# Cross-attention scores from two float32r parts in the 64-row halves of TensorE, in place of three bfloat16 parts in 99 rows

## The chip, the cores and the metric

One core of a Trainium2 chip runs the whole program. The metric is the time of one execution in device microseconds. Three runs of the kernel before gave 1007.08, 1010.96 and 1012.14 us; the median, 1010.96 us, is what the change is measured against.

## What is computed

Two decoder layers on x [2, 512, 256] with a context [2, 1024, 256]. The change touches the two cross-attentions. Cut to them:

```python
# layer 0: keys and values from all 1024 rows of the context, 16 heads of 16
q = split_heads(x_norm @ wq.T + bq); k = split_heads(ctx @ wk.T + bk); v = split_heads(ctx @ wv.T + bv)
p = softmax(where(mask, q @ k.T / 4, -inf)); out = (p @ v) @ wo.T + bo
# layer 1: one key and one value head of 16 for each batch, shared by the 16 query heads,
# from 512 rows of the context, chosen by an exact argmax
p = softmax(q @ k.T / 4); out = (p @ v) @ Wc.T
```

All inputs are float32, and the scores are wanted at nearly float32 accuracy.

## The kernel before

The stages run one after another: Mamba, first cross-attention (`cross_stage`, L1380), experts, shared-key attention, second cross-attention (`hard_cross_stage`, L2112), experts. Both cross-attentions use the class `Attention` (L919).

**Units.** The work is cut into eight units: a batch and a group of four heads (GH = 4). For each unit a query buffer Qs holds 99 partitions x 4 heads x 512 queries in bfloat16, and a key buffer Ks 99 partitions x 4 heads x 1024 keys (in the second attention one head, 512 keys). A float32 number is written as three bfloat16 parts p0 + p1 + p2. The 99 rows are six blocks of 16 (the head's dimensions), which pair the parts so that one matmul sums the six products that matter, and three tail rows, which carry the mask and, in the second pass, minus the row maximum. SyncE fills the blocks by DMA from the part tiles KP and QP (`key_part` L1472, `query_part` L1478) and the tail rows from DRAM or from `ktail` (`tails`, L1465); each DMA counts on the semaphore `loaded`.

**Two passes for each unit.** TensorE makes the scores twice. `scores` (L969, matmul L980) gives 128 queries x 512 keys; VectorE takes the row maxima of each bank (`maxima`, L1075, tensor_reduce L1080). When a unit's maxima are there, `negated` (L1083) writes minus the maximum as two bfloat16 values into MT, TensorE transposes MT (`maxima_transposes`, L1008, L1014), and ScalarE (`tails`, L1152, L1155, heads 0 and 1) and VectorE (`upper_tails`, L1102, L1105, heads 2 and 3) copy the transposed rows into the tail rows of Qs. `transposed_scores` (L984, matmul L992) then gives 128 keys x 512 queries with the maximum already subtracted; ScalarE writes the exponentials to E (L1173), and `values` (L995, L1003) multiplies E by the values of 17 columns, the four heads in the four 32-column groups of TensorE, accumulated over the unit's key tiles in bank 6.

**Order.** `Attention.tensor` writes TensorE's order out by hand. A unit has KT steps (8 in the first attention, 4 in the second), each for a tile of 128 keys. In step kt TensorE issues, for the heads j = 0 to 3 in turn, one `scores` matmul of a later unit and one `transposed_scores` matmul of this one (L1031 to L1038), then the `values` of the step before; in the last step the transposes of the next unit's maxima come ahead of the values, in the second step the transposes of the last unit's output behind them. The scores go round three PSUM banks (MB = 3): score n waits until VectorE has reduced score n - 3. The transposed scores go round three others (XB = 3) in the same way with ScalarE. VectorE's order in a unit is: four reduces a step, in the third step also `normalise` (L1109) of the last unit's output, after the last but one step `negated`, after the last `upper_tails`. Units 0 to 3 of the first attention also make value tiles for the second batch (`late_values`, L1746, two float32 tiles a unit). A prologue ahead of unit 0 makes the scores of unit 0 and the first four of unit 1; the rest of the projections stands between them.

**Before the first scores.** In `cross_stage` a chunk of keys or queries comes out of PSUM as float32, ScalarE rounds it to p0, VectorE or GpSimd subtracts (R), ScalarE rounds R to p1, and VectorE or GpSimd subtracts again (p2); `near` is what unit 0 needs, `far` the rest. SyncE issues two pairs of tail DMAs, and then for unit 0 the blocks of p0, p1 and p2 as they come. `hard_cross_stage` does the same with its queries and, with VectorE, with the 512 keys that it found (`take_found`, L2255), which TensorE transposes (`found_keys`, L2364).

What stands around these places in the code:

## Time and profile before

| | |
|---|---|
| median of three runs | 1010.96 us (1007.08 to 1012.14) |
| span of the profiled execution | 1003.7 us |
| its own time | not given beside its span; the median of the runs is 7.3 us above the span |
| prologue of the first attention | 150.6 to 178.3 us |
| its units 0 to 6 and its last unit | 171.8 us and 27.5 us |
| prologue of the second, its units 0 to 6, its last unit | 19.9, 92.2 and 17.6 us |
| the other stages | about 647 us of the span |

Times in the profile are counted from the start of the span. "L980" is line 980 of the kernel. A timeline's row has the start in us, the length of the merged group, engine, line, operation, tiles and count, and in brackets how long the engine had been idle and who released it. "PE" is TensorE's matmuls, "PEld" its weight loads, "SPq" the DMA issues of SyncE's queue. The length of a matmul is its latency; what the engine can take is read from start to start. A float32 matmul appears as two records.

### The profile page before, as it was taken

What the parts mean: (1) busy time and instruction counts of PE and PEld (TensorE: products, weight loads), DVE (VectorE), ACT (ScalarE), POOL (GpSimd) and SP (SyncE); (2) the same over time, 40 slices, a digit from 0 to 9 for tenths busy, and PEclk for the clock granted to TensorE, in tenths of its full rate; (3) what the DMA queues carried; (4) which work ended last, traced back from release to release, by engine and by line L of the source; (5) the groups of instructions that cost most, each with busy time, mean ns of one, the idle gap of its engine ahead of it and who ended that gap; (6) DMA issues with size and microseconds to landing.
All of it is one profiled execution on the core that took longest, in us unless ns stands there. A gap on an engine that the chain in (4) does not pass through costs nothing. (4 is left out here: it accounts for less than half of the span.)

```text
span 1003.7 us, 12848 instructions
## 1 busy us (share of the span) xinstructions
PE 915.3 (91%) x4110; PEld 459.1 (46%) x4110; DVE 642.4 (64%) x1323; ACT 468.3 (47%) x928; POOL 322.9 (32%) x328
## 2 busy tenths in 40 slices
PE   5889879999999986799999999999988999859996
PEld 2445545333323235366755555555432332534565
DVE  5866558888899823455245555655689897444654
ACT  3886444677777771112133333332216777342321
POOL 7326646200000000166235545554230000115923
PEclk9999998999999997799899999999998999969999
DMA  5040036022223803633491000000200010066200
GB/s 154 1 157 0 1 61 107 1 50 49 49 50 96 289 1 112 242 105 116 144 394 40 1 0 1 1 1 1 65 17 2 32 33 1 1 246 200 75 17 27
DMA packets 41654, 73.79 MB, mean 74 GB/s; under 512 B 8964, under 2 KB 27780, under 8 KB 40436
## 3 DMA queue, kind: packets, MB, share of 16 engines
q1 hardware_dynamic: 36372, 59.68, 19.4%
q0 software_dynamic: 4400, 13.11, 4.1%
q8 instruction: 35, 0.57, 0.2%
q10 hardware_dynamic: 816, 0.17, 0.1%
q14 instruction: 31, 0.25, 0.1%
HBM read 49.67 MB, written 10.49 MB: 60 GB/s over the span
## 5 line engine op out<-in xcount | busy, mean ns | idle before, releaser
L1080 DVE TENSOR_REDUCE c_amx<-PS 128x1 f32<-128x512 f32 x256 | 159.1, 682 | 27.4 <-PE PS L980 27.1
L1173 ACT ACTIVATE c_aE<-PS 128x512 f32<-128x512 f32 x256 | 132.5, 602 | 47.1 <-PE PS L992 46.9
L1835 POOL TENSOR_SCALAR s_Pn<-s_Pr,s_rs 128x512 f32<-128x512 f32 x64 | 100.1, 1566 | 101.5 <-DVE s_rs L1863 101.2
L71 POOL TENSOR_SCALAR rstd<-mv 128x4 f32<-128x4 f32 x8 | 1.9, 233 | 335.5 <-DVE mv L94 335.5
L980 PE MATMUL PS<-c_aKs,c_aQs 99*128 99x512 bf16 x256 | 96.4, 387 | 5.1 <-DMA c_aQs<-area 3.6
L1922 ACT ACTIVATE s_Pr<-PS,s_nmx 128x512 f32<-128x512 f32 x64 | 44.0, 688 | 116.2 <-DVE s_nmx L1856 116.2
L992 PE MATMUL PS<-c_aQs,c_aKs 99*128 99x512 bf16 x256 | 94.5, 380 | 3.5 <-ACT c_aE L1173 2.3
L1854 DVE TENSOR_REDUCE s_mx<-PS 128x1 f32<-128x512 f32 x64 | 44.3, 691 | 68.7 <-PE PS L1970 68.7
L1080 DVE TENSOR_REDUCE h_amx<-PS 128x1 f32<-128x512 f32 x128 | 79.6, 682 | 8.8 <-PE PS L980 8.5
L1173 ACT ACTIVATE h_aE<-PS 128x512 f32<-128x512 f32 x128 | 67.7, 600 | 21.8 <-PE PS L992 21.4
L1003 PE MATMUL PS<-c_aE,c_VB 128*17 128x512 f32 x512 | 67.4, 598 | 0.1
L1970 PE MATMUL PS<-s_KT,s_QT 128*128 128x512 f32 x128 | 65.6, 594 | 1.0 <-ACT s_QT L1907 0.7
L1988 PE MATMUL PS<-s_PT,s_V 128*128 128x512 f32 x128 | 65.7, 595 | 0.3 <-ACT s_OT L1913 0.3
L980 PEld LDWEIGHTS PS<-c_aKs,c_aQs 99*128 99x128 bf16 x256 | 24.9, 98 | 79.0 <-DVE c_amx L1080 55.4
L3179 PE MATMUL PS<-area,g_XsT 128*128 x120 | 56.7, 617 | 0.5 <-ACT g_XsT L3116 0.5
L980 PE MATMUL PS<-h_aKs,h_aQs 99*128 99x512 bf16 x128 | 49.8, 397 | 7.7 <-DVE h_amx L1080 7.1
L1870 DVE COPY s_PT<-PS 128x512 f32<-128x512 f32 x64 | 44.2, 690 | 10.9 <-PE PS L1978 10.9
L992 PE MATMUL PS<-h_aQs,h_aKs 99*128 99x512 bf16 x128 | 48.7, 392 | 2.1 <-ACT h_aE L1173 1.2
L1978 PEld LDWEIGHTS PS<-ident,s_Pn 128*128 128x128 f32 x256 | 31.9, 141 | 32.5 <-issue 26.1
L3121 ACT ACTIVATE g_H<-g_H 128x1024 f32<-128x1024 f32 x15 | 15.9, 1058 | 53.0 <-DVE g_H L3055 53.0
L992 PEld LDWEIGHTS PS<-c_aQs,c_aKs 99*128 99x128 bf16 x256 | 24.6, 98 | 32.2 <-ACT c_aE L1173 9.6
L1978 PE MATMUL PS<-ident,s_Pn 128*128 128x128 f32 x256 | 38.4, 273 | 0.0
(440 smaller groups left out, 1696.8 us busy)
## 6 DMA issues: line engine op xcount, KB each, us to landing
area<-in_e_w SPq DMA_DIRECT2D x16, 512.0 KB, 9.5
area<-in_g_w SPq DMA_DIRECT2D x8, 1024.0 KB, 17.1
c_aKs<-area SPq DMA_DIRECT2D x48, 128.0 KB
g_B<-in_g_b SPq DMA_DIRECT2D x1, 4096.0 KB, 14.3
c_aQs<-area SPq DMA_DIRECT2D x48, 64.0 KB
h_aQs<-h_QP SPq DMA_DIRECT2D x48, 64.0 KB
early<-in_ctxT SPq DMA_DIRECT2D x2, 1024.0 KB, 8.6
e_B<-in_e_b SPq DMA_DIRECT2D x1, 2048.0 KB
```

Of the source, the lines that this page charges most:

```text
L980: pe.matmul(PS[:, n % MB, :], self.Qs[u % self.NQ][:, j, qt * P:(qt + 1) * P], self.Ks[self.key_buffer(u)][:, j % self.KH, half * BANK:(ha ...
L992: pe.matmul(PS[:, MB + n % XB, :], self.Ks[self.key_buffer(u)][:, j % self.KH, kt * P:(kt + 1) * P], self.Qs[u % self.NQ][:, j, :], start= ...
L1003: last = pe.matmul(PS[32 * j:32 * j + VW, 6, :], self.V[:, self.value_unit(u), kt, j % self.KH, :], self.E[kt % 2][:, j, :], start=(kt == ...
L1080: dve.tensor_reduce(self.mx[:, qt, j, half:half + 1], PS[:, n % MB, :], AX.X, ALU.max).then_inc(self.max_done, 1)
L1173: act.activation(self.E[kt % 2][:, j, :], PS[:, MB + x % XB, :], ACT.Exp, scale=0.25).then_inc(self.exp_done, 1)
L1835: pool.tensor_scalar(Pn[g % NPB][:, :], Pr[g % NPB][:, :], rs[:, g % NPB:g % NPB + 1], None, ALU.mult).then_inc(pn_ready, 1)
L1854: dve.tensor_reduce(mx[:, g % NPB:g % NPB + 1], PS[:, g % 2, :], AX.X, ALU.max).then_inc(mx_ready, 1)
L1870: dve.tensor_copy(PT[n % 2][:, :, qt * P:(qt + 1) * P], PS[:, 2 + g % 2, :].rearrange("p (m q) -> p m q", m=TB)).then_inc(pt_ready, 1)
L1970: pe.matmul(PS[:, g % 2, :], QT[n % 2][:, qt * P:(qt + 1) * P], KTr[:, b * S:(b + 1) * S], start=True, stop=True).then_inc(s_mm, 1)
L1978: last = pe.transpose(PS[:, 2 + g % 2, m * P:(m + 1) * P], Pn[g % NPB][:, m * P:(m + 1) * P], sh.ident[:, :])
L1988: last = pe.matmul(PS[:, 5, :], V[:, n // H * TB + m, :], PT[n % 2][:, m, :], start=(m == 0), stop=(m == TB - 1))
L3179: last = pe.matmul(PS[:, 1 + p % 2 * NB1 + half, :], XsT[p % 2][:, k, :], W1[:, k, bass.ds(e * F + half * BANK, BANK)], start=(k == 0), st ...
```

## The change

The change cuts every number into two float32r parts, p0 (the number rounded to float32r) and p1 = x - p0. Three blocks of 16 rows pair them: keys (p0, p0, p1) against queries (p0, p1, p0). With the three tail rows, which now come first, a head has 51 rows. Heads 0 and 2 have theirs in partitions 0 to 50, heads 1 and 3 in 64 to 114. Qs and Ks are float32 of 128 partitions x 2 x n. A matmul of the scores has one head's 51 rows as before it had 99; the transposed scores take the heads in the order 1, 0, 3, 2, so that a `scores` matmul and the transposed one after it lie in different halves. The third parts, the R tiles and ScalarE's second rounding are gone. In each unit SyncE issues 12 block DMAs as before (now two halves x three blocks x two operands, 32 partitions of the source each), and four tail DMAs in place of two in the first attention, two in place of one in the second; the query tails come from a tile in SBUF that one DMA fills first (`load_tail`, which waits for it). The found keys are transposed as float32. The tails' copies now write float32r.

```diff
-NBLK = 6
-TAIL = NBLK * HD
+NBLK = 3
 TAIL_ROWS = 3
-ROWS = TAIL + TAIL_ROWS
+HALF = P // 2
+ROWS = TAIL_ROWS + NBLK * HD
+PAIRS_H = GH // 2
+def rows_of_head(j):
+    return slice(j % 2 * HALF, j % 2 * HALF + ROWS)
+def slot_rows(h, slot):
+    first = h * HALF + TAIL_ROWS + slot * HD
+    return slice(first, first + HD)
...
-        self.Qs = [sb(f"Qs{n}", [ROWS, GH, S], BF16) for n in range(NQ)]
-        self.Ks = [sb(f"Ks{n}", [ROWS, KH, NK], BF16) for n in range(NKB)]
+        self.KP = (KH + 1) // 2
+        self.Qs = [sb(f"Qs{n}", [P, PAIRS_H, S], F32R) for n in range(NQ)]
+        self.Ks = [sb(f"Ks{n}", [P, self.KP, NK], F32R) for n in range(NKB)]
...
+    def load_tail(self, sp, q_tail):
+        sp.dma_start(self.first_tail[:, :], q_tail).then_inc(self.tail_in, 16)
+        sp.wait_ge(self.tail_in, 16)
+    def first_tails(self, sp, u):
+        for h in range(2):
+            sp.dma_start(self.Qs[u % self.NQ][tail_of_head(h), :, :].bitcast(F32).rearrange("r h n -> r (h n)"),
+                         self.first_tail[:, :]).then_inc(self.loaded[u % self.NQ], 16)
...
-            pe.matmul(PS[:, n % MB, :], self.Qs[u % self.NQ][:, j, qt * P:(qt + 1) * P],
-                      self.Ks[self.key_buffer(u)][:, j % self.KH, half * BANK:(half + 1) * BANK],
+            r = rows_of_head(j)
+            pe.matmul(PS[:, n % MB, :], self.Qs[u % self.NQ][r, j // 2, qt * P:(qt + 1) * P],
+                      self.Ks[self.key_buffer(u)][r, j // 2 % self.KP, half * BANK:(half + 1) * BANK],
                       start=True, stop=True).then_inc(self.s_done, 1)
...
-        def transposed_scores(u, kt, j):
+        def transposed_scores(u, kt, x):
-            n = (u * KT + kt) * GH + j
+            n = (u * KT + kt) * GH + x
+            j = x ^ 1
+            r = rows_of_head(j)
...
-            pe.matmul(PS[:, MB + n % XB, :], self.Ks[self.key_buffer(u)][:, j % self.KH, kt * P:(kt + 1) * P],
-                      self.Qs[u % self.NQ][:, j, :], start=True, stop=True).then_inc(self.st_done, 1)
+            pe.matmul(PS[:, MB + n % XB, :], self.Ks[self.key_buffer(u)][r, j // 2 % self.KP, kt * P:(kt + 1) * P],
+                      self.Qs[u % self.NQ][r, j // 2, :], start=True, stop=True).then_inc(self.st_done, 1)
...
-                dve.tensor_copy(self.Qs[u % self.NQ][TAIL:ROWS, j, :],
+                dve.tensor_copy(self.Qs[u % self.NQ][tail_of_head(j), j // 2, :],
                                 PS[32 * j:32 * j + TAIL_ROWS, 7, :].bitcast(BF16)[:, 0:S]
...
-KEY_SLOTS = ((0, 3, 5), (1, 4), (2,))
-QUERY_SLOTS = ((0, 1, 2), (3, 4), (5,))
+KEY_SLOTS = ((0, 1), (2,))
+QUERY_SLOTS = ((0, 2), (1,))
...
+            at.load_tail(sp, A["q_tail"])
             for u in range(2):
                 tails(u)
             at.sync(sp, load, projection_weights)
...
             act.wait_ge(q_mm, 1)
-            act.activation(part("q", 0, 0), bank("q", 0), ACT.Identity, bias=bq[:, 0:1]).then_inc(p0_ready, 1)
-            act.wait_ge(r_ready, 2)
-            act.activation(part("k", 1, 1), RK[1], ACT.Copy).then_inc(p1_ready, 1)
-            act.wait_ge(q0_taken, 1)
-            act.activation(part("q", 0, 1), RQ, ACT.Copy).then_inc(p1_ready, 1)
+            act.activation(rounded("q", 0, 0), bank("q", 0), ACT.Identity, bias=bq[:, 0:1]).then_inc(p0_ready, 1)
             take_transposed(1)
             for i in range(4):
                 far_first(i)
-                if i > 0:
-                    far_second(i - 1)
```

## Rows read from the trace of the kernel before

**Rows 1.** The page's first part: busy time, share of the span, instructions.

```profile
PE 915.3 (91%) x4110; PEld 459.1 (46%) x4110; DVE 642.4 (64%) x1323; ACT 468.3 (47%) x928; POOL 322.9 (32%) x328
```

**Rows 2.** Windows: prologue, steady part and last unit of the first; steady second.

```profile
150.60:178.30 27.70, 26.01 (x89) 13.95 (x89) 24.97 (x42) 12.36 (x25) 15.37 (x14) 0.90 0.61 96
178.30:350.10 171.80, 170.81 (x964) 55.19 (x964) 148.87 (x267) 128.48 (x251) 6.24 (x9) 1.00 0.32 85
350.10:377.60 27.50, 24.52 (x144) 8.27 (x141) 6.56 (x18) 19.20 (x39) 1.27 (x2) 1.00 0.00 1
757.30:849.50 92.20, 87.31 (x489) 28.04 (x489) 82.93 (x165) 70.39 (x132) 0.00 (x0) 0.96 0.06 18
```

**Rows 3.** Timeline, VectorE, one unit: start, us, [idle before <- releaser].

```profile
305.06 2.48 DVE L1080 TENSOR_REDUCE c_amx<-PS 128x1 f32<-128x512 f32 x4
307.76 2.48 DVE L1080 TENSOR_REDUCE c_amx<-PS 128x1 f32<-128x512 f32 x4 [0.21 <-PE PS L980]
311.06 2.48 DVE L1080 TENSOR_REDUCE c_amx<-PS 128x1 f32<-128x512 f32 x4 [0.81 <-PE PS L980]
...
314.08 2.47 DVE L1080 TENSOR_REDUCE c_amx<-PS 128x1 f32<-128x512 f32 x4
316.77 2.48 DVE L1080 TENSOR_REDUCE c_amx<-PS 128x1 f32<-128x512 f32 x4 [0.21 <-PE PS L980]
319.58 2.48 DVE L1080 TENSOR_REDUCE c_amx<-PS 128x1 f32<-128x512 f32 x4 [0.34 <-PE PS L980]
...
325.46 2.48 DVE L1080 TENSOR_REDUCE c_amx<-PS 128x1 f32<-128x512 f32 x4
...
328.89 2.48 DVE L1080 TENSOR_REDUCE c_amx<-PS 128x1 f32<-128x512 f32 x4
```

**Rows 4.** Timeline, all engines, TensorE's rows of one plain step.

```profile
316.34 0.39 PE L980 MATMUL PS<-c_aKs,c_aQs 99*128 99x512 bf16 x1
...
317.51 0.10 PEld L980 LDWEIGHTS PS<-c_aKs,c_aQs 99*128 99x128 bf16 x1 [0.20 <-DVE c_amx L1080]
317.64 0.38 PE L980 MATMUL PS<-c_aKs,c_aQs 99*128 99x512 bf16 x1
...
317.86 0.38 PE L992 MATMUL PS<-c_aQs,c_aKs 99*128 99x512 bf16 x1
...
318.17 1.05 PE L1003 MATMUL PS<-c_aE,c_VB 128*17 128x512 f32 x8
...
319.15 0.39 PE L980 MATMUL PS<-c_aKs,c_aQs 99*128 99x512 bf16 x1
```

**Rows 5.** Timeline, TensorE: weight loads of transposes, plain float32 matmuls.

```profile
310.14 0.42 PEld L1027 LDWEIGHTS PS<-ident,c_aOraw 128*128 128x128 f32 x4 [0.85 <-issue]
...
739.26 3.60 PE L2360 MATMUL PS<-ctx_T,hq_QF 128*128 128x512 f32 x8
```

**Rows 6.** Groups by form, VectorE: busy us, mean ns | idle before.

```profile
L1870 DVE COPY s_PT<-PS 128x512 f32<-128x512 f32 x64 | 44.2, 690 | 10.9 <-PE PS L1978 10.9
...
L1105 DVE COPY c_aQs<-PS 3x512 bf16<-3x512 bf16 x16 | 6.8, 427 | 1.8 <-PE PS L1014 1.4
```

**Rows 7.** Timeline, SyncE's issues before the first scores, and the wait.

```profile
134.67 0.26 SPq L1466 DMA_DIRECT2D c_aQs<-in_q_tail  x1
...
137.39 0.77 SPq L1469 DMA_DIRECT2D c_aKs<-area  x1
139.29 1.93 SPq L1476 DMA_DIRECT2D c_aKs<-area  x3
...
146.78 0.59 SPq L1482 DMA_DIRECT2D c_aQs<-area  x1
...
150.60 1.01 PE L980 MATMUL PS<-c_aKs,c_aQs 99*128 99x512 bf16 x2 [3.60 <-DMA c_aQs<-area]
```

**Rows 8.** Timeline, SyncE, first and last row of unit 7's load.

```profile
307.46 0.26 SPq L1466 DMA_DIRECT2D c_aQs<-in_q_tail  x1
...
319.97 0.36 SPq L1507 DMA_DIRECT2D router<-in_e_small  x1
```

More of the change, by code:

```diff
@@ L9 @@
 F32 = mybir.dt.float32
+F32R = mybir.dt.float32r
 BF16 = mybir.dt.bfloat16
@@ L1167, in step @@
                 n = u * KT + kt
-                for j in range(GH):
-                    x = n * GH + j
+                for i in range(GH):
+                    x, j = n * GH + i, i ^ 1
                     act.wait_ge(self.st_done, x + 1)
-                    if n >= 2 and j == 0:
+                    if n >= 2 and i == 0:
                         act.wait_ge(self.av_done, n - 1)
@@ L1396, in cross_stage @@
     VB = sb("VB", [P, UNITS, KT, GH, VW])
-    loads = 1 + sum(map(len, KEY_SLOTS)) + 1 + sum(map(len, QUERY_SLOTS))
+    loads = 2 * (1 + sum(map(len, KEY_SLOTS)) + 1 + sum(map(len, QUERY_SLOTS)))
     at = Attention(nc, ctx, stage, PS, "c_a", NK, GH, sh.ident, sh.identb, loads)
@@ L1435, in taken @@
         elif (what, n) == ("q", 0):
-            eng.wait_ge(q0_taken, 1)
+            eng.wait_ge(p1_ready, len(near))
         else:
@@ L1445, in part, with rounded @@
         return QP[p][:, m, b * S:(b + 1) * S]
+    def rounded(what, n, p):
+        return part(what, n, p).bitcast(F32R)
     def value_rows(t):
@@ L1486, in load @@
                     pair = [("k", 2 * (u // 2)), ("k", 2 * (u // 2) + 1), ("q", u // 2)]
-                    sp.wait_ge(far_p2_ready, 1 + max(far.index(c) for c in pair))
+                    sp.wait_ge(far_p1_ready, 1 + max(far.index(c) for c in pair))
                     tails(u)
-                for p in range(3):
+                for p in range(2):
                     if u == 0:
-                        sp.wait_ge((p0_ready, p1_ready, p2_ready)[p], 2)
+                        sp.wait_ge((p0_ready, p1_ready)[p], 2)
                     key_part(u, p)
                     if u == 0:
-                        sp.wait_ge((p0_ready, p1_ready, p2_ready)[p], len(near))
+                        sp.wait_ge((p0_ready, p1_ready)[p], len(near))
                     query_part(u, p)
@@ L1565, in _ @@
                 dve.wait_ge(p0_ready, n + 1)
-                dve.tensor_tensor(RK[n], FK[n], part("k", n, 0), ALU.subtract).then_inc(r_ready, 1)
+                dve.tensor_tensor(rounded("k", n, 1), FK[n], part("k", n, 0), ALU.subtract).then_inc(p1_ready, 1)
             at.set_ones(dve)
             dve.wait_ge(p0_ready, 3)
-            dve.scalar_tensor_tensor(out=RQ, in0=bank("q", 0), scalar=bq[:, 0:1], in1=part("q", 0, 0), op0=ALU.add,
-                                     op1=ALU.subtract).then_inc(q0_taken, 1)
-            for i, (c, r) in enumerate(zip(near, RK + [RQ])):
-                dve.wait_ge(p1_ready, i + 1)
-                dve.tensor_tensor(part(*c, 2), r, part(*c, 1), ALU.subtract).then_inc(p2_ready, 1)
+            dve.scalar_tensor_tensor(out=rounded("q", 0, 1), in0=bank("q", 0), scalar=bq[:, 0:1], in1=part("q", 0, 0),
+                                     op0=ALU.add, op1=ALU.subtract).then_inc(p1_ready, 1)
             for n in range(2, 5):
@@ L1601, in far_first @@
                 first_part(far[i], F[i % 4])
-            def far_second(i):
-                act.wait_ge(far_r_ready, i + 1)
-                act.activation(part(*far[i], 1), R[i % 4], ACT.Copy).then_inc(p1_ready, 1)
             def take_queries(n):
@@ L1655, in _ @@
             far_first(8)
-            far_second(7)
-            for t in (4, 5):
-                take_values(t)
-            far_second(8)
-            for t in (6, 7):
+            for t in range(4, KT):
                 take_values(t)
@@ L2128, in hard_cross_stage @@
     NQ = 4
-    loads = 1 + sum(map(len, QUERY_SLOTS))
+    loads = 2 * (1 + sum(map(len, QUERY_SLOTS)))
     at = Attention(nc, ctx, stage, PS, "h_a", S, 1, sh.ident, sh.identb, loads, NQ, B)
     at.V, at.value_unit, at.key_buffer = V, lambda u: u // NG, lambda u: u // NG
+    at.first_tail = sb("first_tail", [TAIL_ROWS, PAIRS_H * S])
     ctxT = sh.context.ctxT
-    QP = [sb(f"QP{n}", [P, KD, T], BF16) for n in range(3)]
-    R = [at.E[1][:, n, :] for n in range(KD * B)]
+    QP = [sb(f"QP{n}", [P, KD, T]) for n in range(2)]
     top = sb("top", [P, NT, 8])
@@ L2167, in key_bank @@
     def key_bank(b):
[L2168 removed]
+        return PS[:, (3, 7)[b], :]
     with stage, nc.Block() as block:
@@ L2192, in _ @@
                     sp.wait_ge(at.av_done, (u - NQ + 1) * at.KT)
-                    tails(u)
-                for p in range(3):
+                    at.first_tails(sp, u)
+                for p in range(2):
                     if n == 0:
-                        sp.wait_ge((p0_ready, p1_ready, p2_ready)[p], 1)
+                        sp.wait_ge((p0_ready, p1_ready)[p], 1)
                     else:
-                        sp.wait_ge(far_p2_ready, n)
+                        sp.wait_ge(far_p1_ready, n)
                     query_part(u, p)
@@ L2312, in _ @@
                 first_part(n)
-            for n in range(KD):
-                second_part(n)
             for k in range(KD):
@@ L2321, in _ @@
             take_keys(0)
-            for n in range(KD, NQC):
-                second_part(n)
             def during(act, u, kt):
@@ L3263, in layouts @@
     A["m_wout"] = ktile(I["L0_attn_out_proj_w"].T)
-    one = 0x3F80
-    A["q_tail"] = np.repeat(np.array([[0], [0], [one]], np.uint16), GH * S, 1)
+    A["q_tail"] = np.repeat(np.array([[0], [0], [1]], np.float32), PAIRS_H * S, 1)
     A["ctxT"] = I["ctx_1024"].transpose(2, 0, 1).reshape(KD, P, -1).transpose(1, 0, 2)
```

143 lines of the change are left out of this document (62 added, 81 removed).

## The prediction, made before the changed kernel ran

> **What bounds the kernel now.** The page's first part says TensorE 91% busy against 64% for VectorE [rows 1], and the table of windows says the same of the stretches that the change touches [rows 2]. That is latency, not rate: a score matmul lasts 0.38 us, but the next can start 0.22 us after it (317.64 and 317.86 [rows 4]). So I read the steps from start to start. In a plain step VectorE's first reduces start 2.81 us apart (316.77 and 319.58 [rows 3]), of which four reduces are 2.48 us and 0.33 us a wait for the scores. The step turns as a loop through two engines [rows 4]: VectorE starts reducing score 0 at 316.77; that bank comes free and lets score 3 load at 317.51, 0.74 us on; it runs at 317.64, when the matmul before it lets it in; the transposed score follows 0.22 us later; the values 0.31 us after that; the next score 0 at 319.15, 0.98 us on; and VectorE has it at 319.58, 0.43 us on. On TensorE alone that is seven times 0.22 (316.34 to 317.86), 0.31 and 0.98, 2.81 us: the plain step is TensorE's, by 0.33 us over VectorE.
>
> Not all steps are plain. The clean unit of rows 3 takes 23.83 us (305.06 to 328.89). Two steps are plain, 2.81. One takes 3.30, because TensorE also transposes an output (307.76 to 311.06, wait 0.81). The two after a delay of VectorE take 2.70 and 2.69 (305.06, 314.08), wait 0.21. Three are VectorE's own, without a wait: with `normalise` 3.02 (311.06 to 314.08), with `negated` (322.40, a row like the plain ones, to 325.46) 3.06, with `upper_tails` 3.43 (325.46 to 328.89). So a clean unit holds 0.33 x 2 + 0.81 + 0.21 x 2 = 1.9 us of waits that a faster TensorE could take back, seven units 13 us. In the second attention a unit has half the steps (92.20 us for seven, 13.2 each [rows 2]): the two steps with waits, 0.21 and 0.81, and the VectorE-bound ones with `upper_tails` and with `negated` and `normalise` together. The last unit of each has no reduces; the loop there is ScalarE's and does not change.
>
> **The change, part by part.** *Rate of the new matmuls.* No row shows float32r. From below it is one pass, 0.22 us as for bfloat16; from above plain float32, where eight records last 3.60 us [rows 5], so about 0.43 a record and, at two records a product, 0.86 us. I take one pass: the rows have the array stream 512 columns in 0.22 us a pass, and four passes are what full float32 takes. The Trainium skill (FP8 and Floating Point Precision, TensorE Precision Notes) says that a float32 can be read at reduced precision, cut to 22 bits, and that true float32 is four passes; no row shows the first half. By it the sum would be the same.
>
> *Two heads in two halves.* Order in a step: score 0 (lower half), transposed 1 (upper), score 1 (upper), transposed 0 (lower), and so on, four pairs in different halves. If a pair overlaps, TensorE's own part of a step falls by nearly four times 0.22, but the loop does not: score 3 still waits for VectorE, 0.74 us after score 0's reduce began. After it: the partner, the values, the next score. The nearest row for overlap is that of the values, four column groups abreast: 8 records in 0.98 us start to start [rows 4] where two in turn take 2 x 0.43 = 0.86, so 0.12 us more for three partners, 0.04 each. The far ends are 0 and 0.14, since four float32 weight loads are (0.42 - 0.14) / 3 = 0.09 us apart [rows 5] and one of them may stand in the way. With 0.04 the new plain step is 0.74 + 0.04 + 0.31 + 0.98 + 0.43 = 2.50 us, against 2.81: 0.31 us less, just above VectorE's 2.48. The Trainium skill (TensorE: Matmul & The Clock Gate, Part 3) has partners start 4 ns apart. By it the plain step would be 2.46 and VectorE the bound.
>
> Per clean unit: plain steps 2 x 0.31; the output step 3.30 to 2.50 + 0.49 + 0.10, 0.21; the two late ones 0.20 and 0.19; together 1.22 us. The 0.10 is a switch of the array's layout: scores now use halves, transposes the whole, and the one switch that rows show, scores to values, costs 0.31 - 0.22 = 0.09 [rows 4]. The Trainium skill (TensorEngine Tiling (Array Packing), Key Properties) says that a change of mode drains TensorE; the 0.09 agrees with it, and it speaks against this change, which adds such switches at outputs, maxima and in the prologues.
>
> *Tail copies.* VectorE's two in a unit go bfloat16 to float32r instead of to bfloat16. Bounds: 427 ns as now, 690 ns as a float32 copy of as many elements [rows 6]. I take 690, as only the form with 16 bits at both ends is fast in these rows: 0.5 us a unit, on VectorE's chain where it has no slack. The Trainium skill (VectorE: DVE Perf Modes, mode 2x_1P) asks for 16-bit types for the fast mode. By it the higher value holds. ScalarE's two copies stay, but both must be done before the first transposed score (head 1 first); VectorE is then in its own copies, so nothing is added.
>
> So a clean unit gains 1.22 - 0.5 = 0.7 us; seven give 5.0. The four units with late value tiles gain 0.1 more each, 0.5. A unit of the second attention gains 0.21 + 0.20 - 0.5 = -0.1; seven give -0.6.
>
> *Start of the first attention.* First scores run at 150.60 after 3.60 us of waiting for DMA [rows 7], so SyncE's queue is on the path. It had finished its tails at 138.16 and waited until 139.29 for p0, and its last block went out at 146.78. New: the load of the tail tile, which SyncE waits for (bounded below by 0.26, its issue; I take 2 us), then four more issues in the place of none (8 tail DMAs for 4, 0.3 to 0.8 each, [rows 7]), so the tails end near 141. Then 12 blocks of 0.63: 148.5 for an end in place of 147.4. The parts are no longer late (one rounding and one subtraction less on ScalarE and VectorE, hidden behind this queue). I take 1.0 us lost; ends: 1 us gained, if half as many packets land faster, and 3 us lost, if the landing slips by all that the first block does.
>
> *At nothing.* Less rounding on ScalarE and GpSimd: both wait most of the prologue (12.4 and 15.4 busy of 27.7 [rows 2]). Prologues: pairs save about what their switches cost, -1 to +1. Unit loads: unit 7's takes 12.5 us (307.46 to 319.97 [rows 8]); two more issues make it 13.7, and VectorE has its first scores at 325.46 [rows 3], 18 us after its start, some 17 after the change. If this cover went, each unit would stall. Memsets and float32 transposes of found keys: TensorE is behind with context scores there.
>
> **The sum.** 5.0 + 0.5 - 0.6 - 1.0 = 3.9 us saved: a span of 999.8 for 1003.7. The median is 7.3 us above the profiled span, so 1007.0 for 1010.96, or 0.4%. This kernel's measurement can tell about 0.5%, 5 us, from no change. Ends: with free overlap, the tail copies at 427 ns and no loss at the start some 14 us, and 16 with the prologues; with the partner at 0.14, slow copies, a late start and prologues, 4 us lost.
>
> **Rivals.** *VectorE's floor is reached* (997): overlap free and tail copies as before. Units: 1.4 us each in the first attention, 0.5 in the second, 9.9 + 0.5 + 3.4 = 13.8. For it: the values' four groups do overlap. Against: only the 16-bit copy is fast [rows 6].
>
> *No overlap of halves* (1017.5). float32r at one pass, but pairs run in turn. Then 2.81 stays, the tail copies cost 0.5 less the 0.21 wait behind them in 14 units, 4.1, the switches 1.4, the start 1.0: 6.5 us slower. For it: all score matmuls here are in turn, and no row has two row groups at work. Against: the values.
>
> *Several passes: slower* (1160). The place is each score matmul. Two passes in overlapped pairs: 3 x 0.43 to score 3, 0.04, 0.43 + 0.09, 0.98 make 2.83 us, so the gain ends there; from there on it costs. Four: 3 x 0.86 + 0.04 + 0.95 + 0.98 = 4.55 a step, 13 us a unit and 5.6 in the second attention, 130 in all, and about 20 in prologues and last units. For it: this is what the only 4-byte matmuls in the trace take [rows 5]. Against: only that those work out full float32, and this type needn't.
>
> *The clock falls.* A TensorE that works less may be granted 1.2 GHz in place of 2.4. In the second attention's units the clock is at 0.96 after a thin prologue [rows 2]. At half clock the streamed parts of the loop (two scores, the values, about 1.3 us) double: 3.8 a step, 80 us if it lasted throughout (1090). Against: the last unit of the first attention, with 4 x 0.22 + 0.98 of work in about 2.4 us, ran at 1.00 [rows 2]; the changed step streams as much in 2.50.
>
> **Chances.** Forecast 0.64 (0.29 over 5 us faster, 0.33 within, 0.02 slower), VectorE's floor 0.12 (faster), no overlap 0.12 (half within, half slower), several passes 0.07, clock 0.05 (both slower). Faster 0.41, same 0.39, slower 0.20. The range, 996 to 1020, takes in the first three cases with their bounds and leaves out the last two and some tails.
>
> **What would show it.** Right: score and transposed score starting under 0.1 us apart in pairs; plain steps near 2.50; c_aQs copies by VectorE at about 690 ns; VectorE's waits in a clean unit down from 1.9 to under 1 us; first scores at 151 to 152; clock 1.00. Wrong: matmuls of a pair 0.22 apart (no overlap), records over 0.43 us or two a product (passes), granted clock under 1.00 in the units, or the queue of unit loads ending a wait of TensorE.

## The result: 2.5% slower, and the profile after

The changed kernel takes 1032.12 us (median of four, 1029.32 to 1039.59) against 1009.02 us (four runs, 1005.81 to 1012.14) for the kernel before; the ratio on record is 1.025, 95% interval 1.022 to 1.029 (the two medians alone give 1.023). An execution more than 1.5% above the fastest of its kernel is left out below; there was one, in run 3 (1050.31 us). The forecast was 1007.0 us, its range ended at 1020. The profiled execution has a span of 1028.5 us and took 1030.3 us.

The page's first part, which answers to [rows 1]:

```profile
PE 906.2 (88%) x4110; PEld 469.1 (46%) x4110; DVE 648.8 (63%) x1315; ACT 459.9 (45%) x912; POOL 310.5 (30%) x317
```

Busy time hides what happened: TensorE is busy for less time, and weight loads grew by 10 us, as the float32r ones take twice as long. The table of windows says where the time is; its stretches answer to [rows 2] in their order (prologue, units 0 to 6, last unit of the first attention; units 0 to 6 of the second), and the last columns are the granted clock, the DMA share and GB/s:

```profile
153.30:185.60 32.30, 31.05 (x88) 13.47 (x88) 25.18 (x42) 8.85 (x18) 7.54 (x6) 0.84 0.47 83
185.60:365.40 179.80, 157.67 (x963) 59.46 (x964) 152.66 (x267) 130.00 (x251) 6.26 (x9) 0.95 0.34 82
365.40:395.70 30.30, 25.79 (x140) 9.93 (x142) 7.08 (x18) 18.86 (x37) 1.27 (x2) 0.94 0.00 1
777.50:873.50 96.00, 81.16 (x489) 30.57 (x488) 85.70 (x163) 69.86 (x132) 0.00 (x0) 0.95 0.08 18
```

Cut at the same instructions in both traces (first scores, first maxima transposes, last values), the 24.8 us of span are:

| stretch | before | after | more |
|---|---|---|---|
| start of the span to the first scores | 150.6 | 153.3 | 2.7 |
| prologue, first attention | 27.7 | 32.3 | 4.6 |
| units 0 to 6 | 171.8 | 179.8 | 8.0 |
| last unit | 26.8 | 30.3 | 3.5 |
| experts and shared-key attention | 361.0 | 360.7 | -0.3 |
| prologue, second attention | 19.7 | 21.1 | 1.4 |
| units 0 to 6 | 91.9 | 96.0 | 4.1 |
| last unit | 16.9 | 18.1 | 1.2 |
| rest | 137.3 | 136.9 | -0.4 |

**One clean unit.** VectorE's timeline, which answers to [rows 3] (start, us, and in brackets how long the engine had been idle):

```profile
292.09 2.48 DVE L1110 TENSOR_REDUCE c_amx<-PS 128x1 f32<-128x512 f32 x4
294.59 1.41 DVE L1135 CAST c_aQs<-PS 3x512 fp32r<-3x512 bf16 x2
296.04 2.48 DVE L1110 TENSOR_REDUCE c_amx<-PS 128x1 f32<-128x512 f32 x4
298.80 2.48 DVE L1110 TENSOR_REDUCE c_amx<-PS 128x1 f32<-128x512 f32 x4 [0.28 <-PE PS L1008]
302.08 2.48 DVE L1110 TENSOR_REDUCE c_amx<-PS 128x1 f32<-128x512 f32 x4 [0.79 <-PE PS L1008]
...
305.10 2.47 DVE L1110 TENSOR_REDUCE c_amx<-PS 128x1 f32<-128x512 f32 x4
307.78 2.48 DVE L1110 TENSOR_REDUCE c_amx<-PS 128x1 f32<-128x512 f32 x4 [0.21 <-PE PS L1008]
310.48 2.48 DVE L1110 TENSOR_REDUCE c_amx<-PS 128x1 f32<-128x512 f32 x4 [0.21 <-PE PS L1008]
313.18 2.48 DVE L1110 TENSOR_REDUCE c_amx<-PS 128x1 f32<-128x512 f32 x4 [0.22 <-PE PS L1008]
...
316.25 2.48 DVE L1110 TENSOR_REDUCE c_amx<-PS 128x1 f32<-128x512 f32 x4
```

The unit lasts 316.25 - 292.09 = 24.16 us, 0.33 more than in [rows 3]. Its step with the tail copies is 3.95 (292.09 to 296.04, 3.43 before). Every other step that is not VectorE's own still has its wait: 0.28, 0.79, 0.21, 0.21, 0.22, together 1.7 us where the prediction left under 1. A plain step is 2.70, neither the 2.81 of before nor the 2.50 of the forecast.

**One plain step.** The timeline of TensorE and its weight loads, which answers to [rows 4]:

```profile
231.06 0.49 PE L1008 MATMUL PS<-c_aKs,c_aQs 51*128 51x512 f32 x1
...
231.06 0.72 PE L1022 MATMUL PS<-c_aQs,c_aKs 51*128 51x512 f32 x2
...
231.59 2.48 DVE L1110 TENSOR_REDUCE c_amx<-PS 128x1 f32<-128x512 f32 x4 [0.21 <-PE PS L1008]
...
231.63 0.39 PE L1022 MATMUL PS<-c_aQs,c_aKs 51*128 51x512 f32 x1
...
232.33 0.18 PEld L1008 LDWEIGHTS PS<-c_aKs,c_aQs 51*128 51x128 f32 x1 [0.71 <-DVE c_amx L1110]
232.34 0.50 PE L1008 MATMUL PS<-c_aKs,c_aQs 51*128 51x512 f32 x1 [0.32 <-DVE c_amx L1110]
...
232.34 0.50 PE L1022 MATMUL PS<-c_aQs,c_aKs 51*128 51x512 f32 x1
...
232.77 1.05 PE L1033 MATMUL PS<-c_aE,c_VB 128*17 128x512 f32 x8
233.75 0.18 PEld L1008 LDWEIGHTS PS<-c_aKs,c_aQs 51*128 51x128 f32 x1 [0.85 <-DVE c_amx L1110]
...
234.28 1.29 DVE L1110 TENSOR_REDUCE c_amx<-PS 128x1 f32<-128x512 f32 x2 [0.21 <-PE PS L1008]
```

The overlap is there: a score and its transposed partner start within 0.01 us, which is what the Trainium skill (TensorE: Matmul & The Clock Gate, Part 3) has for tiles in different rows. Around the loop: VectorE starts at 231.59; score 3 at 232.33, 0.74 later; the partner at once; the values 0.43 after score 3 (forecast 0.04 + 0.31); the next score 0 at 233.75, 0.98 later; VectorE at 234.28, 0.53 later (forecast 0.43). Sum 2.69. Both links that grew begin with a weight load that nothing covers: the load and its matmul start together (232.33 and 232.34; 233.75 both), and the record is 0.50 us. Where the load was made under an earlier matmul, the float32r record is 0.39 (231.63), as long as bfloat16's. The groups by form give load and latency (busy us, mean ns), after:

```profile
L1022 PE MATMUL PS<-c_aQs,c_aKs 51*128 51x512 f32 x256 | 95.4, 472 | 7.0 <-ACT c_aE L1203 4.3 <-ACT c_aQs L1185 1.6 <-DVE c_aQs L1135 0.2
...
L1008 PEld LDWEIGHTS PS<-c_aKs,c_aQs 51*128 51x128 f32 x256 | 42.4, 195 | 106.5 <-DVE c_amx L1110 85.5 <-issue 17.5
L1135 DVE CAST c_aQs<-PS 3x512 fp32r<-3x512 bf16 x16 | 11.0, 690 | 2.2 <-PE PS L1044 1.7
```

The load of before takes 0.10 us in [rows 4] and its matmul 0.38. Plain float32 weights of 128 columns took 190 ns already in the trace of before:

```profile
L2360 PEld LDWEIGHTS PS<-ctx_T,hq_QF 128*128 128x128 f32 x64 | 11.8, 190 | 15.7 <-issue 13.9 <-ACT hq_QF L2293 1.5 <-DVE h_idx L2250 0.2
```

The Trainium skill (TensorE: Matmul & The Clock Gate, Weight-path perf modes) says that 128 columns of a type other than float32 are loaded by a faster way. It does not say on which side float32r falls; these rows put it with float32 (195 ns beside 190, and about 100 for bfloat16). The prediction did not weigh this rule.

**The start.** SyncE's issues answer to [rows 7]:

```profile
134.81 0.25 SPq L972 DMA_DIRECT2D area<-in_q_tail  x1
136.46 1.61 SPq L977 DMA_DIRECT2D c_aQs<-area  x2
...
142.68 2.61 SPq L1509 DMA_DIRECT2D c_aKs<-area  x4
...
149.13 1.23 SPq L1517 DMA_DIRECT2D c_aQs<-area  x2
```

and TensorE's rounds behind them (two scores, then a float32 chunk):

```profile
153.32 0.79 PE L1008 MATMUL PS<-c_aKs,c_aQs 51*128 51x512 f32 x2 [6.17 <-DMA c_aQs<-area]
...
156.05 0.79 PE L1008 MATMUL PS<-c_aKs,c_aQs 51*128 51x512 f32 x2
```

TensorE now waits 6.17 us for the DMA where it waited 3.60 [rows 7], and works at half clock behind it: a round of 2.73 us. The kernel before did so too, but for 6.8 us (149.5 to 156.3) where this one has 13.7 (149.7 to 163.4).

### The profile page after: what moved, and what is told of

It reads as the page before. It is cut to its first block and busy times, and to the rows that moved or that the text cites. A ratio compares the mean times of both kernels' runs of the same rounds, so it can differ in the third digit from the quotient of the medians.

```text
span 1028.5 us, 12833 instructions
## 1 busy us (share of the span) xinstructions
PE 906.2 (88%) x4110; PEld 469.1 (46%) x4110; DVE 648.8 (63%) x1315; ACT 459.9 (45%) x912; POOL 310.5 (30%) x317
## 3 DMA queue, kind: packets, MB, share of 16 engines
q0 software_dynamic: 4400, 13.11, 4.1%
## 5 line engine op out<-in xcount | busy, mean ns | idle before, releaser
L1203 ACT ACTIVATE c_aE<-PS 128x512 f32<-128x512 f32 x256 | 134.6, 602 | 57.1 <-PE PS L1022 55.6
L1008 PE MATMUL PS<-c_aKs,c_aQs 51*128 51x512 f32 x256 | 94.4, 477 | 26.6 <-DVE c_amx L1110 19.0
L1022 PE MATMUL PS<-c_aQs,c_aKs 51*128 51x512 f32 x256 | 95.4, 472 | 7.0 <-ACT c_aE L1203 4.3
L1008 PEld LDWEIGHTS PS<-c_aKs,c_aQs 51*128 51x128 f32 x256 | 42.4, 195 | 106.5 <-DVE c_amx L1110 85.5
L1033 PE MATMUL PS<-c_aE,c_VB 128*17 128x512 f32 x512 | 71.1, 628 | 0.0
L1008 PE MATMUL PS<-h_aKs,h_aQs 51*128 51x512 f32 x128 | 48.4, 471 | 15.9 <-DVE h_amx L1110 14.2
L1022 PE MATMUL PS<-h_aQs,h_aKs 51*128 51x512 f32 x128 | 48.0, 479 | 4.7 <-ACT h_aE L1203 2.4
L1022 PEld LDWEIGHTS PS<-c_aQs,c_aKs 51*128 51x128 f32 x256 | 42.4, 193 | 21.3 <-ACT c_aE L1203 10.6
L1008 PEld LDWEIGHTS PS<-h_aKs,h_aQs 51*128 51x128 f32 x128 | 21.4, 194 | 51.2 <-DVE h_amx L1110 41.2
```

Of the source, the lines that this page charges most:

```text
L1008: pe.matmul(PS[:, n % MB, :], self.Qs[u % self.NQ][r, j // 2, qt * P:(qt + 1) * P], self.Ks[self.key_buffer(u)][r, j // 2 % self.KP, half ...
L1022: pe.matmul(PS[:, MB + n % XB, :], self.Ks[self.key_buffer(u)][r, j // 2 % self.KP, kt * P:(kt + 1) * P], self.Qs[u % self.NQ][r, j // 2, ...
L1033: last = pe.matmul(PS[32 * j:32 * j + VW, 6, :], self.V[:, self.value_unit(u), kt, j % self.KH, :], self.E[kt % 2][:, j, :], start=(kt == ...
L1203: act.activation(self.E[kt % 2][:, j, :], PS[:, MB + x % XB, :], ACT.Exp, scale=0.25).then_inc(self.exp_done, 1)
```

## The experiments

The runs of the kernel before beside them have medians of 1008.0 to 1009.5 us. One thing is left out in some of these kernels, and is said here once: where both parts are bfloat16 (four runs), an operand is kept to some 16 bits, as there is no third part.

**1. bfloat16 in the halves.** Separates float32r from the layout.

```diff
-        self.Qs = [sb(f"Qs{n}", [P, PAIRS_H, S], F32R) for n in range(NQ)]
-        self.Ks = [sb(f"Ks{n}", [P, self.KP, NK], F32R) for n in range(NKB)]
+        self.Qs = [sb(f"Qs{n}", [P, PAIRS_H, S], BF16) for n in range(NQ)]
+        self.Ks = [sb(f"Ks{n}", [P, self.KP, NK], BF16) for n in range(NKB)]
...
-    KP = [area.take([P, B, KD, NK]) for _ in range(2)]
-    QP = [area.take([P, KD, T]) for _ in range(2)]
+    KP = [area.take([P, B, KD, NK], BF16) for _ in range(2)]
+    QP = [area.take([P, KD, T], BF16) for _ in range(2)]
```

> The changed kernel with bfloat16 in place of float32r in all operands of the scores (two parts, so 16 bits of the scores instead of about 22; layout, order and DMAs as in the change). Theory A: the loss is the 4-byte type: its weight load of 183 ns (98 ns before) stands twice in the loop of a plain step, its tail copy is 0.69 us, and the tail DMAs delay the start. Then the plain step here is 0.74 + 0.01 + 0.31 + 0.98 + 0.43 = 2.47, say 2.5 us, VectorE's copies are 0.43 us, a clean unit takes 22.6 us (23.8 before, 24.15 in the change), the start stays 2 to 3 us late: 1008 to 1014 us. Theory B: the loss is the overlap, which leaves TensorE thin, so that its clock falls: here TensorE is thinner still, the granted clock stays at 0.95 or less in the units, and the time is above 1020 us.

Measured: 1005.62 us, ratio 0.998 (0.995 to 1.001), level with the kernel before and 2 us under the range of Theory A. VectorE's timeline and the loads by form:

```profile
289.94 9.90 DVE L1110 TENSOR_REDUCE c_amx<-PS 128x1 f32<-128x512 f32 x16
...
302.93 0.88 DVE L1135 COPY c_aQs<-PS 3x512 bf16<-3x512 bf16 x2
```

```profile
L1008 PE MATMUL PS<-c_aKs,c_aQs 51*128 51x512 bf16 x256 | 79.0, 397 | 28.6 <-DVE c_amx L1110 24.1 <-DMA c_aQs<-area 4.5
L1008 PEld LDWEIGHTS PS<-c_aKs,c_aQs 51*128 51x128 bf16 x256 | 19.2, 94 | 115.5 <-DVE c_amx L1110 97.9 <-issue 16.2
```

Sixteen reduces in 9.90 us: four steps of 2.48 without a wait. The clean unit is 22.64 us (286.92 to 309.56), units 0 to 6 take 166.1. So the plan of the change, halves that overlap, does in the plain steps what the prediction said, down to VectorE's floor; what spoils it is the type. Load 94 ns for 195, latency 397 for 477, and both links are short again: the values start 0.32 us after score 3 (295.63 and 295.95) for 0.43, and VectorE 0.42 after score 0 (309.14 and 309.56) for 0.53. The tail copies are 424 ns again, too, so this run alone does not part the loop from the copies.

**2. No overlap.** Heads in the order 0, 2, 1, 3 in both passes, so that neighbours share a half.

```diff
+ORDER = (0, 2, 1, 3)
+SORDER = (0, 2, 1, 3)
...
+            j = SORDER[j]
             r = rows_of_head(j)
...
-            j = x ^ 1
+            j = ORDER[x]
```

> The changed kernel with scores and transposed scores taken in the order of heads 0, 2, 1, 3, so that a score and the transposed one behind it lie in the same half and hardly overlap. Theory A: the units gain nothing from overlap in the loop but for the partner's 0.2 us, so a plain step goes from 2.69 to 2.9 (0.22 more behind score 3), about 40 of the steps show it: 8 us slower, less what a fuller TensorE gives back in clock (up to 8 us): 1032 to 1040 us. Theory B: with TensorE fuller the clock is at 1.00 in the units as before and the time falls by the 8 us or so that the half clock cost: 1022 to 1028 us.

Measured: 1068.79 us, ratio 1.061 (1.058 to 1.065). Windows: the prologue with the first steps, and units at full clock.

```profile
149.00:218.00 69.00, 63.18 (x118) 27.85 (x120) 31.97 (x52) 14.57 (x28) 13.79 (x15) 0.51 0.29 50
...
218.00:389.00 171.00, 161.50 (x914) 69.93 (x915) 143.30 (x250) 119.93 (x234) 0.00 (x0) 1.00 0.36 87
```

```profile
320.73 2.48 DVE L1113 TENSOR_REDUCE c_amx<-PS 128x1 f32<-128x512 f32 x4
323.65 2.48 DVE L1113 TENSOR_REDUCE c_amx<-PS 128x1 f32<-128x512 f32 x4 [0.43 <-PE PS L1011]
```

Neither theory had this size. In the steps it is as the trace of the change says: in one half score 3 starts at 321.48 and its transposed partner at 321.82, 0.34 apart for 0.01, and a plain step is 2.92. But most of the loss is the clock: from the wait for the DMA on it stayed at the lower level for 68 us (150.7 to 218.9), though TensorE has records over 63 of the 69 us of the first window. The prologue took 55.3 us. Why the clock did not rise was not found.

**3. Tails later.** Undoes the wait and the tail DMAs ahead of unit 0's blocks.

```diff
-            at.load_tail(sp, A["q_tail"])
-            for u in range(2):
-                tails(u)
+            sp.dma_start(at.first_tail[:, :], A["q_tail"]).then_inc(at.tail_in, 16)
+            key_tails(0)
+            sp.wait_ge(at.tail_in, 16)
+            at.first_tails(sp, 0)
```

> The changed kernel with unit 1's four tail DMAs behind unit 0's blocks, and unit 0's key tails ahead of the wait for the query tail. SyncE's last block for unit 0 goes out at 146.9 in place of 150.4. Theory A: first scores at 150 (153.3 in the change, 150.6 before), and with TensorE's wait of 6.2 us back near 3 the stretch at half clock before and in the prologue shrinks: 5 to 7 us less in all, 1025 to 1027 us. Rival: the data, not the queue, is late; then the first scores come less than 1 us earlier and the time stays at 1031 or 1032.

Measured: 1038.38 us (three executions, 1030.32 to 1041.36), ratio 1.028 (1.020 to 1.035): neither theory. In the trace the start is as wanted: the last block goes out at 149.3 although the queue's first DMA went out 2.2 us later than in the changed kernel (136.97 for 134.81), and TensorE waits 2.85 us for the DMA in place of 6.17.

```profile
152.15 0.79 PE L1008 MATMUL PS<-c_aKs,c_aQs 51*128 51x512 f32 x2 [2.85 <-DMA c_aQs<-area]
```

The total shows nothing of it. The clock fell all the same in that wait, and the prologue took 32.3 us again. Two more stretches of 10.2 us at half clock go with the rest: one from 527.4, in the stages between the attentions (366.6 us for 360.7), and one in the second attention's last unit (21.9 us for 18.1). Why they came was not found.

**4. TensorE kept busy.** 16 spare matmuls ahead of the first scores, and one transposed score of each step made twice.

```diff
+            if x == 2:
+                for _ in range(FILL):
+                    pe.matmul(PS[:, MB + n % XB, :], self.Ks[self.key_buffer(u)][r, j // 2 % self.KP, kt * P:(kt + 1) * P],
+                              self.Qs[u % self.NQ][r, j // 2, :], start=True, stop=True)
...
             pe.wait_ge(xT_ready, KD * B)
+            spare_matmuls(pe, sh, 0, 16)
```

> The changed kernel with idle TensorE filled: 16 spare matmuls of 512 columns before the first scores, and in every step the third transposed score is made twice, its first copy 0.23 us ahead where TensorE waits for VectorE anyway. Theory A: the clock is at 1.00 in units and prologue, the loop of the plain step stays 2.69, and the time falls by the price of the half clock, 2 to 3 us in the first prologue and 5 to 7 us in units and last units: 1022 to 1026 us. Rival: the clock's falls follow the waits at unit boundaries, which this doesn't fill; then the granted clock of the units stays at 0.95 and the time within 3 us of 1032.

Measured: 1030.65 us, ratio 1.021 (1.017 to 1.025). Units 0 to 6 of the first attention take 176.3 us for 179.8, at a clock of 0.98 for 0.95:

```profile
188.00:359.90 171.90, 161.97 (x996) 66.22 (x996) 149.42 (x260) 126.69 (x244) 6.27 (x9) 0.98 0.36 84
```

The unit from 290.99 is 24.15 us, with plain steps of 2.70, as in the changed kernel: the extra matmul costs nothing there, TensorE's own streaming is not the bound, and the 3.5 us less go with the clock (6.8 us at half clock for 17.0). The total lies between the two theories. At the start the spare matmuls ended at 153.0, 2.65 us before the scores could begin, and the prologue fell to half clock for 10.2 us all the same.

**5. Tail copies to ScalarE.** Three of four there, one on VectorE.

```diff
-            for j in range(GH // 2, GH):
+            for j in (3,):
                 dve.tensor_copy(self.Qs[u % self.NQ][tail_of_head(j), j // 2, :],
...
-            for j in range(GH // 2):
+            for j in (1, 0, 2):
                 act.activation(self.Qs[u % self.NQ][tail_of_head(j), j // 2, :],
```

> The changed kernel, but ScalarE makes three of the four tail copies of a unit (heads 1, 0, 2) and VectorE one (head 3). Theory A (the 690 ns copies lie on VectorE's chain, where it has no slack): a clean unit falls from 24.15 us by one copy, 0.69, to about 23.5, a unit of the second attention from 13.68 to about 13.0, and the kernel by 14 x 0.69, some 9 us, to 1023, ratio 1.014. Rival B (TensorE's loop, stretched by the slower weight load, takes it back): the steps behind the copies are TensorE's by then, the wait in them grows from 0.21 by as much as VectorE comes earlier, and the unit stays within 0.2 us of 24.15: the kernel at 1030 to 1033.

Measured: 1030.36 us, ratio 1.021 (1.017 to 1.024). VectorE's timeline:

```profile
311.60 2.48 DVE L1112 TENSOR_REDUCE c_amx<-PS 128x1 f32<-128x512 f32 x4
314.11 0.70 DVE L1137 CAST c_aQs<-PS 3x512 fp32r<-3x512 bf16 x1
314.83 2.48 DVE L1112 TENSOR_REDUCE c_amx<-PS 128x1 f32<-128x512 f32 x4
318.02 2.48 DVE L1112 TENSOR_REDUCE c_amx<-PS 128x1 f32<-128x512 f32 x4 [0.70 <-PE PS L1008]
```

The step with the copy fell from 3.95 to 3.23, and the next one rose from 2.76 to 3.19, its wait from 0.28 to 0.70: the unit is 23.87 us (290.96 to 314.83), 0.29 less and not 0.69. Rival B, nearly; but the place is ScalarE. Its three copies last until 315.33,

```profile
313.52 1.81 ACT L1187 ACTIVATE c_aQs<-PS 3x512 fp32r<-3x512 bf16 x3
315.36 2.06 ACT L1205 ACTIVATE c_aE<-PS 128x512 f32<-128x512 f32 x4
```

the exponentials come behind them, and in TensorE's order the last transposed score (316.10) and the values (316.50) stand ahead of VectorE's next score (317.48). Units 0 to 6 took 173.8 us, 6.0 less than in the changed kernel: 2.0 are 7 x 0.29, the other 4.0 go with 3.4 us at half clock where that trace has 17.0.

**6. The three mends together.** Edits 3, 4 and 5.

> The changed kernel with the three mends together: three tail copies on ScalarE, the first query tails of unit 1 behind unit 0's blocks, and spare matmuls (16 before the first scores, one more transposed score in each step). Theory A (the loss is a sum of terms that stand apart): start 3.3 less, tails 9 less, clock 3.5 less than the changed kernel's 1032: some 1016, ratio 1.008; what is left over the kernel before is the prologue (about 3), and the wait behind a plain step, 2.70 where bfloat16 has 2.48. Rival B (the terms stand in for one another: the spare matmul takes TensorE's slack, so that what VectorE gains turns into waits): 1024 to 1030.

Measured: 1025.94 us (1017.87 to 1030.74), ratio 1.019 (1.015 to 1.023): 6 us of 23 come back, Rival B's size. The profiled execution is the fastest of them, and shows what clock and start are worth:

```profile
152.40:180.30 27.90, 26.66 (x90) 12.44 (x89) 25.00 (x42) 8.85 (x18) 7.55 (x6) 1.00 0.58 108
180.30:354.00 173.70, 164.69 (x1020) 67.84 (x1020) 148.07 (x260) 133.59 (x258) 6.27 (x9) 0.99 0.36 85
```

Here the spare matmuls led straight into the scores (two mends that worked only together: runs 3 and 4 each had 10.2 us at half clock there), the clock stayed at 1.00, and the prologue took 27.9 us for 32.3.

**7 and 8. The bfloat16 form with the mends.** Run 7 adds to run 1 the later tails and the 16 spare matmuls, run 8 also ScalarE's tail copies.

> The halves with bfloat16 parts (two parts in place of three, so a coarser score), with the later query tails at the start and 16 spare matmuls ahead of the first scores. Against the same without them (1005.6, ratio 0.998): theory A (start queue and clock are terms of their own): start 3.3 less, the prologue's half clock (10.2 us, some 2.5 lost) gone: 1000, ratio 0.992. Rival B (the half clock comes back at another place, as it did when it left the first scores in the run with spare matmuls and float32r): 1003 to 1005.

> The kernel of the run beside it (bfloat16 parts in halves, later tails, spare matmuls) and three tail copies on ScalarE. In this form VectorE has no wait in the plain steps, so what leaves it must leave the unit. Theory A: each unit shorter by the one copy, 0.44 us (clean unit 22.64 to 22.2), 14 units: 6 us less than the run beside it, about 994 to 997. Rival B (ScalarE's three copies of 0.58 us delay the first transposed scores and with them the exponentials, whose engine is then the later one): no gain, within 1 us of the run beside it.

Measured: run 7 1005.56 us, ratio 0.997 (0.995 to 0.999); run 8 1002.47 us, ratio 0.994 (0.992 to 0.996). Run 7 is Rival B, nearly: the prologue is 26.5 us for 28.5 and starts 1.1 us earlier, but 10.2 us at half clock behind it stay (from 177.2) and the median is that of run 1. In run 8 a unit starts at 296.47 as follows:

```profile
298.98 0.43 DVE L1137 COPY c_aQs<-PS 3x512 bf16<-3x512 bf16 x1
299.44 2.48 DVE L1112 TENSOR_REDUCE c_amx<-PS 128x1 f32<-128x512 f32 x4
302.57 2.48 DVE L1112 TENSOR_REDUCE c_amx<-PS 128x1 f32<-128x512 f32 x4 [0.65 <-PE PS L1008]
```

The copy's 0.45 us came back as a wait of 0.65, as in run 5, the unit is 22.79 us (296.47 to 319.26) for 22.64, and units 0 to 6 took 165.6 us for 166.1: Rival B by the trace. The median is 3 us lower than run 7's, inside both spreads (999 to 1008 each).

**9. Maxima from the upper halves.** The scores that only serve the maxima read the upper 16 bits of the same tiles.

```diff
+def upper(x):
+    return x.bitcast(BF16)[:, 1::2]
...
-            pe.matmul(PS[:, n % MB, :], self.Qs[u % self.NQ][r, j // 2, qt * P:(qt + 1) * P],
-                      self.Ks[self.key_buffer(u)][r, j // 2 % self.KP, half * BANK:(half + 1) * BANK],
+            pe.matmul(PS[:, n % MB, :], upper(self.Qs[u % self.NQ][r, j // 2, qt * P:(qt + 1) * P]),
+                      upper(self.Ks[self.key_buffer(u)][r, j // 2 % self.KP, half * BANK:(half + 1) * BANK]),
```

> The changed kernel, but the scores that only serve the maxima read the upper 16 bits of each operand as bfloat16 (every other 16-bit word), so these maxima are those of rounded scores; the transposed scores, from which the exponentials come, stay float32r. Theory A (the plain step's 2.70 is the float32r load of 0.18 us and the 0.49 us latency behind it, twice in the loop): the load of score 0 falls to 0.09 and its record to 0.38, VectorE has it 0.43 after its start, and the plain step falls by 0.10 to about 2.59; score 3's partner is still float32r, so the values stay 0.42 behind it. A clean unit falls from 24.15 to about 23.7, the kernel by 5 us to 1027. Rival B (it is the transposed score next to it that holds TensorE's weight port, or reading every other word costs as much as 4 bytes do): 2.69 and 1032 as before it. Rival C (a change of type between partners ends their overlap): plain step 2.9 and over 1040.

Measured: 1023.83 us (1022.5 to 1031.81), ratio 1.017 (1.012 to 1.022). The maxima's loads by form (195 ns in the changed kernel) and VectorE's timeline:

```profile
L1012 PEld LDWEIGHTS PS<-c_aKs,c_aQs 51*128 51x128 bf16 x256 | 22.8, 95 | 106.3 <-DVE c_amx L1114 81.3 <-issue 17.9
```

```profile
298.20 10.27 DVE L1114 TENSOR_REDUCE c_amx<-PS 128x1 f32<-128x512 f32 x16
```

Theory A, nearly to the digit: sixteen reduces in 10.27 us, 2.57 a step; unit from 289.25 to 313.01, 23.76 us. With nothing changed but how one of the two matmuls reads its operands, one of the two longer links (VectorE after score 0: 0.44, 291.47 to 291.91, for 0.53) shortened, and the other (values 0.42 after score 3, by the partner that is still float32r) did not: score 3 at 231.59, the values at 232.01. That shows the cause of the plain step: the 0.10 us of a link is the 0.10 us of the load. The type next to it does not end the overlap (Rival C).

**10. The same with the three mends.**

> The maxima from the upper 16 bits, together with the three mends (tails on ScalarE, later query tails at the start, spare matmuls). The run with the three mends alone gave 1025.9 (its profiled execution 1017.9). Theory A: 0.10 less in each step with a wait, five of eight in a unit of the first attention and most in the second, 14 units: 5 us less, 1021, ratio 1.013. Rival B (no effect of the type of the maxima's operands): 1024 to 1028.

Measured: 1014.23 us (1011.28 to 1018.97, ten runs), ratio 1.006 (1.004 to 1.009). More than Theory A gave: the prologue is also shorter, 26.6 us for 27.9; its scores now all have the short load. It is the best form with float32r, and still slower than before.

**11. Run 8 with a score made twice in each step.**

> The fastest form so far (bfloat16 parts in halves, later tails, 16 spare matmuls, three tail copies on ScalarE: 1002.5) with one transposed score of each step made twice. Theory A (half clock in and around the units, 10 us in the first attention and 13 us in the second, costs 0.35 us per us, and a TensorE that works more keeps its clock): 3 to 4 us less, 999. Rival B (the second score stands in the loop, 0.22 us a step, and the plain step passes VectorE's 2.48): clean unit above 22.6, the kernel at 1005 or more.

Measured: 1002.23 us, ratio 0.994 (0.991 to 0.997), the same as run 8; units 0 to 6 took 166.9 us for 165.6, and the half clock at the prologue's end stayed (10.2 us from 178.6, for 6.8 in run 8). Neither theory: the second score costs nothing in the loop, and buys no clock.

**12. The kernel before with the spare matmuls.**

> The kernel before with nothing but 16 spare matmuls ahead of its first scores: does the gain of the bfloat16 forms come from these? Theory A (the 6.8 us at half clock from 148.5 cost the first round some 2 us, and the spare matmuls cover the wait of 3.6 us for the DMA): ratio 0.998. Rival B (they end before the wait does, the clock falls all the same): ratio 1.000. A ratio at or under 0.995 would say that the halves bring nothing.

Measured: 1006.33 us, ratio 0.998 (0.996 to 1.000): the value of Theory A, though the interval reaches 1.000. The trace decides for it:

```profile
152.40:177.60 25.20, 23.41 (x89) 12.98 (x90) 24.60 (x42) 12.49 (x25) 15.50 (x15) 1.00 0.63 106
```

The prologue of before at full clock is 25.2 us for 27.7. Of run 8's 0.6%, then, some 0.2% may be the spare matmuls' and not the halves'. This row also splits the changed kernel's prologue: at a clock of 1.00 it is 27.9 (run 6), 2.7 more than 25.2; the other 1.9 of its 4.6 us are the clock.

## Why the prediction was wrong

**Right.** One record for each score matmul, so no several passes. Partners start together: the prediction took 0.04 us for one, the trace has 0.01. VectorE's copies take 690 ns, so 0.5 us a unit (3.43 to 3.95). The DMA loads of the later units end no wait of TensorE. Given bfloat16's load, the loop comes down to VectorE's 2.48 (run 1).

**The step that failed: 0.31 and 0.43 in the sum of the plain step.** The prediction bounded the passes of float32r, but took both links over from bfloat16's rows, as if the type had no other price than its passes. Each begins with a weight load that nothing covers, and each came out 0.08 to 0.10 us above the forecast: 0.04 + 0.31 became 0.43, 0.43 became 0.53. (Why the load of score 0 is not made earlier, under the values, was not looked into; with bfloat16 it isn't either.) The step is 0.74 + 0.43 + 0.98 + 0.53, about 2.69, and the gain of 0.31 shrinks to 0.12. The same 0.2 us keep the waits of the late steps (0.21, forecast none) and of the output step (3.28, forecast 3.09). A clean unit gained 1.22 in the sum; it gained 0.2 and paid the 0.5 of the copies: +0.33, 2.3 us in seven. In the second attention a unit is 13.68 us for 13.11, 4.0 in seven (forecast 0.1 a unit lost, 0.6 in all). The trace of before had the warning, in the row of L2360 above: 190 ns for a float32 load. The prediction looked only at the four loads of a transpose in [rows 5] (0.42 us, a mean of 140 ns each), and used them for the partner alone.

**Last units, held to be unchanged.** Their loop holds a waiting transposed score and its load too: 2.60 a step for 2.38 (values at 380.00 and 382.60), 8 x 0.22 = 1.8 us in the first attention and 0.9 in the second, of 3.5 and 1.2. The first also has 3.4 us at half clock (from 371.6), where the kernel before had none; that share was not separated.

**Prologues, set at -1 to +1.** 4.6 and 1.4 us. The first is 2.7 at full clock: a round of two scores and a float32 chunk has a pitch of 1.49 us in run 6, 1.30 in run 12. The bfloat16 halves have 1.38, so 0.11 is for the load and 0.08 for the layout, in sixteen rounds. What the 0.08 is made of shows in run 7: the two scores run at once, so the chunk starts 0.32 us after them (169.34 and 169.66; 0.44 in run 12), but the next scores start 1.07 after the chunk (170.73) where run 12 has 0.86. The way back into the halves costs 0.21, more than the 0.12 that the pair saves, and the prediction had 0.09 for such a switch. The Trainium skill (TensorEngine Tiling (Array Packing), Key Properties), which the prediction held against the change, says that a change of mode drains TensorE; the 0.21 agrees with it, no run shows the drain itself. The 1.4 of the second prologue was not split.

**Start, set at 1.0.** 2.7. The wait for the tail tile was 1.65 us, as sized (2), and the twelve blocks take 0.64 each, as sized. But the eight tail DMAs take 0.78 each (136.46 to 142.68), at the upper end of the 0.3 to 0.8 given: they end at 142.6 and not at 141, and the last block goes out at 150.4 (forecast 148.5). Run 3 shows it the other way round: out of the way, they give back 3.3 us of the wait.

**The clock, a rival with 0.05.** It came in part: 0.95 in the units of both attentions, where the kernel before had 1.00 and 0.96. In units 0 to 6 of the first, 17.0 us at half clock go with 5.7 of the 8.0 us (8.0 - 2.3); run 5, with 3.4 us of it, has 4.0 less than its copies explain, and run 4, with 6.8 us and the same clean unit, 3.5 less: about a third of a us for each us at half clock. That it falls rather with less work for TensorE in a unit's first step is only argued: in the changed kernel a wait of 0.85 us for ScalarE's tails stands at 187.3, where such a stretch begins, but run 11's extra work did not lift it. The prediction priced only a clock that stays down throughout (1090 us), and not one that falls at the joints.

**Together.** Start 2.7, prologues 2.7 + 1.9 + 1.4, units 2.3 + 5.7 + 4.1, last units 4.7, other stages -0.7: 24.8 us. Of these 2.7 + 1.9 + 5.7, some 10, are the start and the clock; the others, about 15, are put down mostly to a load of 0.18 us in place of 0.10 and to copies of 690 ns in place of 427; run 9 shows the load's part in the plain step, the trace the copies', and the rest of the split is a sum, not an experiment. That all of it goes with the type is shown: run 1, which differs from the changed kernel only in it (and so in the bytes that the DMAs move), is 26 us faster, clock and all. The prediction bounded the rate of float32r from both sides, and its range of 24 us was that of the other terms; an uncovered load had no bound of its own.
